# Query and key products of a linear-attention layer: seven half products in place of eight, the residual parked in memory, loops over pairs written out

## The reference, cut to what matters

```python
H, D, BS = 32, 64, 64
qkv = silu(hidden_states @ qkv_w.T).reshape(b, s, H, 3 * D)
q, k, v = split(qkv, 3)
# per head: attention inside a block with a decay, plus a decayed running state
aw = einsum('bhid,bhjd->bhij', qi, ki) * dd
out = einsum('bhij,bhjd->bhid', aw, vi) + einsum('bhid,bhde->bhie', qi * qd, state)
state = state * bd + einsum('bhsd,bhse->bhde', ki * kd, vi)
attn = rmsnorm(out, norm_w)
gate = sigmoid(hidden_states @ gate_w.T)
return gate * attn @ out_w.T
```

## Time and profile before

| | before |
|---|---|
| median of 3 runs | 5099.79 us (5098.65 to 5100.75) |
| the profiled execution's own time | 5098.89 us |
| its span | 5097.2 us |
| `linear_heads`, first product to last output product | 2950.80 to 4164.5 us of the span |
| PE busy | 4591.1 us, 90% of the span |
| DVE, POOL, ACT busy | 48%, 32%, 32% |
| mean granted TensorE clock | 0.952 of full |

### The profile page before, as it was taken

The page is one execution under the profiler, slowest core; times in us unless marked ns, Lnnn a source line. Parts: engine busy times, 40 slices in busy tenths (PEclk is TensorE's granted clock), DMA queues, the critical chain, the costliest instruction groups (busy, mean ns, idle before and its releaser), DMA issues. The chain is left out here.

```text
span 5097.2 us, 66465 instructions
## 1 busy us (share of the span) xinstructions
PE 4591.1 (90%) x26178; PEld 2569.4 (50%) x26180; DVE 2425.6 (48%) x3642; ACT 1625.0 (32%) x2792; POOL 1638.8 (32%) x1066
## 2 busy tenths in 40 slices
PE   6359997899999999969999689999999989699996
PEld 3124443433333333246666356666665658666663
DVE  7865888367777777751222313333333344512222
ACT  5414443211555556632111122222222210321110
POOL 2010000002888885215555211111111110155553
PEclk8679998999999999989999899999999999899998
DMA  2000000100000000047888610000000022479987
GB/s 74 0 15 7 7 0 35 35 0 1 1 2 1 1 1 1 6 148 222 256 259 258 148 62 32 23 30 32 32 23 31 23 83 88 157 213 257 258 258 195
DMA packets 237588, 417.72 MB, mean 82 GB/s; under 512 B 31472, under 2 KB 119536, under 8 KB 237296
## 3 DMA queue, kind: packets, MB, share of 16 engines
q1 hardware_dynamic: 179952, 270.89, 16.0%
q0 software_dynamic: 57344, 142.64, 11.5%
HBM read 297.53 MB, written 115.93 MB: 81 GB/s over the span
## 5 line engine op out<-in xcount | busy, mean ns | idle before, releaser
L2387 PE MATMUL linb_pr_ps<-lin_z,linb_wt 128*128 128x512 f32 x1536 | 679.4, 596 | 17.0 <-POOL linb_slope_own L2357 17.0
L1557 ACT ACTIVATE attc_prob<-attc_ps 128x512 f32<-128x512 f32 x1024 | 547.8, 597 | 298.9 <-PE attc_ps L1473 288.7
L1589 DVE TENSOR_REDUCE attc_peak<-attc_ps 128x1 f32<-128x512 f32 x768 | 490.5, 682 | 204.8 <-PE attc_ps L1481 204.8
L1444 POOL TENSOR_TENSOR attc_acc<-attc_acc,attc_prob 128x2048 f32<-128x2048 f32 x120 | 543.4, 4528 | 40.3 <-ACT attc_prob L1557 26.4
L1481 PE MATMUL attc_ps<-att_k,att_q 32*128 32x512 f32 x1536 | 492.0, 641 | 0.0
L2387 PEld LDWEIGHTS linb_pr_ps<-lin_z,linb_wt 128*128 128x128 f32 x1536 | 286.9, 192 | 343.5 <-issue 326.3
L1473 PE MATMUL attc_ps<-att_q,att_k 32*128 32x512 f32 x2048 | 459.7, 589 | 0.0
L2563 DVE SCALAR_TENSOR_TENSOR linb_gated<-linb_osb,linb_norm_w,linb_proj 128x512 f32<-128x512 f32 x64 | 94.4, 1474 | 668.0 <-ACT linb_osb L2490 668.0
L2364 POOL TENSOR_TENSOR linb_sq<-linb_osb 128x512 f32<-128x512 f32 x64 | 70.2, 1096 | 1040.5 <-ACT linb_osb L2490 1040.5
L1493 PE MATMUL attc_ps<-attc_prob,att_v 128*32 128x256 f32 (+1 forms) x3472 | 310.4, 429 | 0.4 <-ACT attc_prob L1557 0.4
L1074 DVE TENSOR_TENSOR_SCAN ssmb_state<-ssmb_decay,ssmb_bu 128x2048 f32<-128x2048 f32 x64 | 280.7, 4413 | 54.3 <-PE ssmb_y_ps L927 29.4
(11 more groups left out here) (463 smaller groups left out, 7655.5 us busy)
## 6 DMA issues: line engine op xcount, KB each, us to landing
moe1w_wgu<-in_L_ffn_gate_up_proj SPq DMA_DIRECT2D x32, 1536.0 KB
moe2w_wgu<-in_L_ffn_gate_up_proj SPq DMA_DIRECT2D x32, 1536.0 KB
moe1w_wd<-in_L_ffn_down_proj SPq DMA_DIRECT2D x32, 512.0 KB
gated_features<-linb_gated SPq DMA_DIRECT2D x64, 256.0 KB, 2.3
moe2w_wd<-in_L_ffn_down_proj SPq DMA_DIRECT2D x32, 512.0 KB
linc_gt<-gated_features SPq DMA_DIRECT2D x7, 2048.0 KB, 8.2
linb_wt<-in_L_attn_b_qkv_w SPq DMA_DIRECT2D x16, 768.0 KB, 4.7
residual_rows<-residual SPq DMA_DIRECT2D x8, 1024.0 KB, 4.3
```

Of the source, the lines that this page charges most:

```text
L1444: pool.tensor_tensor(to, before, prob[:, U % NP, :, :], ALU.add).then_inc(pool_done, 2 if at % HALF == 1 else 1)
L1557: nc.scalar.activation(prob[:, U % NP, h, :], ps[:, bank_of(("score", U, h)), :], ACT.Exp).then_inc(exp_done, 1)
L1589: V.tensor_reduce(peak[:, w // TT % 2, i % QH, h, b:b + 1], ps[:, bank_of(("peak", U, h)), :], axis=AX.X, op=ALU.max).then_inc(mx_used, 1)
L2387: last = nc.tensor.matmul(pr_ps[:, use % 2, :], wt[:, b, kind, k, :], z[:, k, t * NB:(t + 1) * NB], start=(k == 0), stop=(k == DT - 1))
```

## The change

Let A be the weights of a pair: two block rows (query weights, key weights) by two block columns (input features 0 to 255, 256 to 511). Let B be the features: two block rows by two block columns (token block 2x, token block 2x+1). Queries and keys of two token blocks are the four blocks of A·B. The code before computes them as eight half products (each two matmuls of 512 columns, four PE records). The code after computes them as seven, by the scheme with four sums on each side (s1 to s4 of weights, t1 to t4 of tokens) and five sums behind.

- The weight sums are four tensor_tensor of 256 columns per pair on POOL, ahead of its squares of quarter 0. The token sums are eight of 1024 columns, once, on DVE. They are kept where `g.X` was: SP writes the residual to DRAM at the start, and reads it back when the last pair's products are done, between the saves of pair 14 and those of pair 15.
- Per x (0, 1): ACT copies p1 out of PSUM and takes one block out with Silu. DVE makes five sums of 512 columns (`u2`, `u3`, `kB`, `kA`, `qB`), each of one PSUM bank and one tile. ACT then applies Silu to three blocks in place, from on-chip memory. PE's products wait for these sums where they reuse or add to a bank.
- `pr_ps` has three banks, `o_ps` one instead of two.
- Quarter 0 carries the value pieces, quarter 1 the gate pieces and the tables, quarters 2 and 3 the seven products for x = 0 and 1 (two ahead of `additions`, five behind). The first quarter of a pair waits for the last in-place Silu.
- All loops over pairs are written out on every engine and SP; waits have constants.

```diff
-        PIECES = KINDS * TC
+        PIECES = 2 * TC + 2 * 7
+        PRODUCTS = ("p1", "p6", "p2", "p7", "p5", "p4", "p3")
+        SUMS = ("u2", "u3", "kB", "kA", "qB")
...
-            with eng.Fori(0, PAIRS_L // 2 - 1) as r:
-                body(r * 2, r, 0, True)
-                body(r * 2 + 1, r, 1, True)
-            body(PAIRS_L - 2, PAIRS_L // 2 - 1, 0, True)
-            body(PAIRS_L - 1, PAIRS_L // 2 - 1, 1, False)
+            for n in range(PAIRS_L):
+                body(n, n // 2, n % 2, n + 1 < PAIRS_L)
...
+            load(0, 0)
+            sp.dma_start(x_rows, g.X[:, :, :]).then_inc(x_spilled, 16)
+            load(1, 1)
...
+                if n + 1 == PAIRS_L:
+                    sp.wait_ge(x_spilled, 16)
+                    sp.wait_ge(pr_done, PAIRS_L * PIECES)
+                    sp.dma_start(g.X[:, :, :], x_rows).then_inc(x_back, 16)
...
+            def weight_sums(n, b):
...
+                pool.tensor_tensor(s1, a21, a22, ALU.add).then_inc(w_summed, 1)
+                pool.tensor_tensor(s3, a11, a21, ALU.subtract).then_inc(w_summed, 1)
+                pool.wait_ge(w_summed, 4 * n + 1)
+                pool.tensor_tensor(s2, s1, a11, ALU.subtract).then_inc(w_summed, 1)
+                pool.wait_ge(w_summed, 4 * n + 3)
+                pool.tensor_tensor(s4, a12, s2, ALU.subtract).then_inc(w_summed, 1)
...
+            def product(bank, left, right, fresh):
+                for k in range(HK):
+                    last = nc.tensor.matmul(pr_ps[:, bank, :], left[:, k, :], right[:, k, :],
+                                            start=(fresh and k == 0), stop=(k == HK - 1), skip_group_check=not fresh)
+                last.then_inc(pr_done, 1)
...
+                if "p1" in some:
+                    pe.wait_ge(pr_out, n * FROM_BANKS + (2 * TC + 2 if x else 2 * TC - 1))
+                    product(one, a11, b11, True)
+                if "p6" in some:
+                    pe.wait_ge(w_summed, 4 * n + 4)
+                    pe.wait_ge(z_summed, 4 * x + 4)
...
+                    product(two, s2, t2, True)
+                if "p2" in some:
+                    pe.wait_ge(pr_out, n * FROM_BANKS + 2 * TC + 2 * x + 1)
+                    product(one, a12, b21, False)
+                if "p7" in some:
+                    pe.wait_ge(added, after_sum(n, x, "u2"))
+                    product(two, s3, t3, False)
+                if "p5" in some:
+                    if x:
+                        pe.wait_ge(added, after_sum(n, 0, "qB"))
+                    product(three, s1, t1, True)
+                if "p4" in some:
+                    pe.wait_ge(added, after_sum(n, x, "u3"))
+                    product(two, a22, t4, False)
+                if "p3" in some:
+                    pe.wait_ge(added, after_sum(n, x, "kB"))
+                    product(three, s4, b22, False)
...
                 for q in range(TC):
                     keys_first(n, b, q)
-                    if more:
-                        piece(q, 0, n + 1, r + b, 1 - b)
+                    if more and q < 2:
+                        piece(q + 2, 0, n + 1, r + b, 1 - b)
+                    elif more:
+                        seven(n + 1, 1 - b, q - 2, PRODUCTS[0:2])
                     additions(n, b, q)
...
+                    elif more:
+                        seven(n + 1, 1 - b, q - 2, PRODUCTS[2:])
                     outputs(n, b, q)
...
+            def seven_out(n, b, x):
+                act.wait_ge(pr_done, after_product(n, x, "p1"))
+                if n or x:
+                    act.wait_ge(added, (2 * n + x) * len(SUMS))
+                nc.scalar.copy(p1[:, :], pr_ps[:, 0, :]).then_inc(pr_out, 1)
+                act.wait_ge(pr_done, after_product(n, x, "p2"))
+                nc.scalar.activation(proj[b][:, 0, tokens(2 * x)], pr_ps[:, 0, :], ACT.Silu).then_inc(pr_out, 1)
+                for name, kind, t in (("kB", 1, 2 * x + 1), ("kA", 1, 2 * x), ("qB", 0, 2 * x + 1)):
+                    act.wait_ge(added, after_sum(n, x, name))
+                    nc.scalar.activation(proj[b][:, kind, tokens(t)], proj[b][:, kind, tokens(t)], ACT.Silu).then_inc(qk_out, 1)
...
+            def sums(n, b, x, some):
+                if "u2" in some:
+                    dve.wait_ge(pr_done, after_product(n, x, "p6"))
...
+                    V.tensor_tensor(u2[:, :], pr_ps[:, 1, :], p1[:, :], ALU.add).then_inc(added, 1)
+                if "u3" in some:
+                    dve.wait_ge(pr_done, after_product(n, x, "p7"))
+                    V.tensor_tensor(u3[:, :], pr_ps[:, 1, :], p1[:, :], ALU.add).then_inc(added, 1)
...
+                    V.tensor_tensor(proj[b][:, 1, tokens(2 * x + 1)], pr_ps[:, 2, :], u3[:, :], ALU.add).then_inc(added, 1)
...
+                    V.tensor_tensor(proj[b][:, 1, tokens(2 * x)], pr_ps[:, 1, :], p1[:, :], ALU.add).then_inc(added, 1)
...
+                    V.tensor_tensor(proj[b][:, 0, tokens(2 * x + 1)], pr_ps[:, 2, :], u2[:, :], ALU.add).then_inc(added, 1)
...
+                    if more and q >= 2:
+                        sums(n + 1, 1 - b, q - 2, ("u2",))
                     update(n, q)
+                    if more and q >= 2:
+                        sums(n + 1, 1 - b, q - 2, SUMS[1:])
```

More of the change, by code:

```diff
@@ L2325, in _ @@
                 sp.dma_start(g.y_dram[1][i * P:(i + 1) * P, :], nothing[:, :]).then_inc(cleared, 16)
[L2326 to L2331, removed]
+            for n in range(PAIRS_L):
+                if n + 2 < PAIRS_L:
+                    reload(n, n % 2)
+                if n + 1 == PAIRS_L:
+                    sp.wait_ge(x_spilled, 16)
+                    sp.wait_ge(pr_done, PAIRS_L * PIECES)
+                    sp.dma_start(g.X[:, :, :], x_rows).then_inc(x_back, 16)
                 for q in range(TC):
-                    save(PAIRS_L - 2 + b, q)
+                    save(n, q)
             for b in range(2):
@@ L2369, in _ @@
             pool.sem_inc(sq_done, 2)
-            over_pairs(pool, body)
+            weight_sums(0, 0)
+            over_pairs(body)
         @block.tensor
@@ L2386, in piece @@
                     for k in range(DT):
-                        last = nc.tensor.matmul(pr_ps[:, use % 2, :], wt[:, b, kind, k, :], z[:, k, t * NB:(t + 1) * NB],
-                                                start=(k == 0), stop=(k == DT - 1))
+                        last = nc.tensor.matmul(bank, wt[:, b, kind, k, :], z[:, k, tokens(t)], start=(k == 0), stop=(k == DT - 1))
                 last.then_inc(pr_done, 1)
+            def product(bank, left, right, fresh):
[3 more added lines that the diff above has]
+                last.then_inc(pr_done, 1)
@@ new lines, in seven @@
+            def seven(n, b, x, some):
+                a11, a12, a22 = wt[:, b, 0, 0:HK, :], wt[:, b, 0, HK:DT, :], wt[:, b, 1, HK:DT, :]
+                b11, b21, b22 = z[:, 0:HK, tokens(2 * x)], z[:, HK:DT, tokens(2 * x)], z[:, HK:DT, tokens(2 * x + 1)]
+                s1, s2, s3, s4 = (wsum[:, j, :, :] for j in range(4))
+                t1, t2, t3, t4 = (zsum[:, x, j, :, :] for j in range(4))
+                one, two, three = range(3)
+                if "p1" in some:
[5 more added lines that the diff above has]
+                    if x:
+                        pe.wait_ge(added, after_sum(n, 0, "kA"))
+                    else:
+                        pe.wait_ge(pr_out, n * FROM_BANKS + 2 * TC)
+                    product(two, s2, t2, True)
[6 more added lines that the diff above has]
+                if "p5" in some:
+                    if x:
+                        pe.wait_ge(added, after_sum(n, 0, "qB"))
[6 more added lines that the diff above has]
+                    product(three, s4, b22, False)
@@ L2440, in _ @@
             pe.wait_ge(consts, N_CONSTS)
-            for kind in range(KINDS):
+            for kind in (2, 3):
                 for t in range(TC):
                     piece(kind, t, 0, 0, 0)
+            for x in range(2):
+                seven(0, 0, x, PRODUCTS)
             def body(n, r, b, more):
@@ L2489, in quarter_out @@
                 act.wait_ge(osb_used, m + 1)
-                nc.scalar.copy(osb[:, q % 2, :], o_ps[:, q % 2, :]).then_inc(o_out, 1)
-            act.sem_inc(pr_out, 2)
+                nc.scalar.copy(osb[:, q % 2, :], o_ps[:, :]).then_inc(o_out, 1)
             act.sem_inc(kt_done, 1)
@@ L2499, in _ @@
             table(0, 0)
-            for kind in range(KINDS):
+            for kind in (2, 3):
                 for t in range(TC):
                     piece_out(kind, t, 0, 0)
+            for x in range(2):
+                seven_out(0, 0, x)
             def body(n, r, b, more):
@@ L2506, in body @@
                     keys_out(n, q)
[L2507 to L2509 removed]
+                    if more and q < 2:
+                        if q == 1 and n:
+                            act.wait_ge(gated_done, n * TC)
                         for t in range(TC):
[L2511 to L2512 removed]
```

(12 more changed lines are left out.)

87 lines of the change are left out of this document (66 added, 21 removed).

## The result

The kernel after takes 5027.99 us (median of 4 runs, 5025.78 to 5029.77) against 5099.22 of before: ratio 0.9858, 95% interval 0.9846 to 0.987. The forecast was 5028. The profiled execution took 5025.78 us, its span is 5024.1, 73.1 less than before. Of the runs further down, one of the kernel with doubled sums took 5381.75 us at a mean granted clock of 0.855, against 0.951 in the others of that kernel, and is left out of its median.

A forecast was written before the change was run, and what follows sets the result against it. PE's instructions were taken to bound the head stage: 5098.89 - 54.9 (products) - 17.3 (loops) + 0.7 (prologue) = 5027.4, plus 0.9 for the median, 5028 us. Own range 5020 to 5040; 8-in-10 range 5018 to 5048.

The forecast's parts named there:

- Products: On PE in the head stage, two half products fewer per pair save 3.43 us, 54.9 us over 16 pairs.
- Loops: PE's hardware-loop turns in the head stage cost 17.3 us, 12.0 of it idle; written-out loops save it all.
- that rival: PE's "issue" gap at loop turns stays in written-out code: 17.3 us come back, 5046 us; chance 0.05.
- End of the prologue: PE's 0.8 us wait before pair 0 is uncovered and grows by one sum, +0.7 us.
- Covers: In seven-product quarters, other PE work hides each wait for sums by 0.5 to 1.7 us; priced zero.
- DVE: Ten sums a pair add 6.9 us to DVE's 23 of now 70 us, not near PE.
- POOL: Four weight sums take about 3 us in quarter 0, needed over 36 us later; price zero.
- Parking: Residual write to DRAM takes 11 us, at most 17, read back ends at 13 to 19; covered, price zero.
- The price of a rate half as high: Rival in the last pair: a read back at half the slow rate holds it, about 12 us, 5040; chance 0.04.
- Quarters: Start to start, quarter 0 takes 19.0 us, quarter 1 18.2, quarters 2 and 3 16.5 each; a pair 70.4.
- Clock: With no gaps on PE, the stage has no lowered-clock stretch but the first; clock 1.00.
- The rival that three cycled banks make the clock swing: Within the small-waits rival: waits of three PSUM banks show as a clock under 1.00; 5060 to 5071, chance 0.08.

The follow-up runs named there:

- the two mixed kernels: Kernel before with PE's loop kept, all others written out: 5100.21 us, ratio 1.000; with PE's loop alone written out: 5082.57 us, ratio 0.9965.
- The kernel with three sums: Kernel after with each of DVE's five sums preceded by two more of the same size: 5080.07 us, ratio 0.9962.

## Why the prediction was right

- *Products*: 54.9 us forecast. Measured 51.6 for 15 pairs by the difference of two kernels, and 54.9 for all 16 by adding the product back.
- *Loops*: 17.3 us forecast from 15 pairs against their undisturbed length; 17.25 measured with the loops alone written out. The gap did not stay, so that rival is excluded. That it is PE's own turn was not known before; the two mixed kernels show it.
- *End of the prologue*: +0.7 forecast; PE's wait there grew from 0.8, for ACT's last piece, to 1.5, for the last in-place Silu.
- *Covers*: all held. I laid them out for the slowest DVE and gave u2 1.0 us to spare; it has 1.5 in the quarter shown: the gating there starts 0.7 us into the quarter and not 1.5, and takes 0.75 and not 1.54, so that u2 waits only for its product. The 0.5 us at the pair boundary is 0.65, of which 0.10 is hand-over, a cost that I took as zero. The kernels with more sums show that these were the margins: the boundary's ends just short of twice the work, the products' between two and three times.
- *DVE*: I took 6.9 us more a pair; it was 4.9 (27.91 against 22.98). The ten sums cost 0.69 each as forecast; the gating was slow less often (last section). Of 160 sums only one ran beside an instruction of POOL, at 692 ns, so that they hold 0.69 beside POOL is hardly tested.
- *POOL*: price zero, right. A weight sum is 722 ns, 2.9 us for four; I said about 3.
- *Parking*: price zero, right, but its sizes were off. I took 11 us, 17 at most; it was 15.6 out and 16.2 back. The rate of 382 GB/s was not what was wrong. On the way out the weights of two pairs were in flight beside the 4 MB, and on the way back the first microseconds are slow (last section). The save of quarter 0 landed 18.8 us into the last pair, and the gating that needs its buffer came at 23.7. The price of a rate half as high, 12 us, was not tested as such; with twice the bytes it was 5.7.
- *Quarters*: I expected 19.0, 18.2, 16.5, 16.5 and got 18.76, 18.42, 16.70, 16.48. The pair's 70.36 was right, but these four add up to 70.2. Quarters 0 and 3 have two records fewer than 1 and 2 (no state product for the first chunk, no update for the last). My 18.2 was a quarter 3, so 1 and 2 came out 0.2 us short. And my 3.63 us for a value piece counted the length of the last record; in the kernel before the quarter with the values takes 18.98 us against 18.42 for the one ahead of it, 0.14 us a piece, so a value piece is 3.57 and quarter 0 came out 0.24 too long.
- *Clock*: no lowered stretch in the pairs, as forecast. The rival that three cycled banks make the clock swing did not come true: 1.00 over 914.68 us. In the kernel after PE has no idle between groups for it to act on. The kernel with three sums has: up to 0.7 us of idle at p4 and at the pair boundary, and its clock from pair 0 to pair 15 is 1.00 too.

## What to carry to other kernels

Where one engine is busy in every microsecond of a stage, price a change as instructions times their start-to-start distance on it, and spend the rest of the work on whether each new wait has another instruction of that engine in front of it. Take the loss of a hardware loop as the difference between the real and the undisturbed length of its passes: it holds the idle turn and the clock that falls behind it. Written-out code matters on the engine that sets the pace; on the others it changed nothing here. Do not take the time of one transfer from issue to landing as the time of the next: what else is in the queues and the slow start are in it, and the second of two transfers can cost less.

## What the runs showed of the hardware

- PE's loop turn costs 1.8 to 2.4 us of idle, 12.0 in six, and in three of six turns a quarter at a granted clock of 0.91 behind it, 1.6 us more. Which turns differ from run to run, and the length of the gap does not decide it: in the kernel before a gap of 1.81 us had a slow quarter behind it (19.81), one of 2.23 had none (18.20). The total was the same 17.3 in the kernel before and with the others' loops written out.
- 15.6 and 16.2 us from issue to landing are not the rate of a 4 MB transfer. On the way out, 365 GB/s moved from 2935.5 to 2951.0, the weights of two pairs included, and 406 to 411 from 2940. On the way back, 216 GB/s from 4065 to 4068 and 402 from 4071 to 4074. Of the two reads issued back to back the second landed 11.4 us behind the first, 367 GB/s; the clearing moved at 382.
- DVE's gating and POOL's square read the same tile at nearly the same moment, and one of the two is slow each time. Before, POOL starts at 3443.60 and takes 1.04, DVE at 3443.65 takes 1.54. After, DVE starts at 3553.44 and takes 0.75, POOL at 3553.55 takes 1.54. The Trainium skill, SBUF — State Buffer, "Who interferes with whom", says that whoever issues first holds the shared ports for the whole instruction and blocks the other; these rows agree. By the start times that the profile records it does not always come out so. In 44 of the 128 gatings of both kernels DVE starts 43 to 45 ns ahead of POOL and is the slow one all the same:

```profile
3025.80 1.63 DVE L2698 SCALAR_TENSOR_TENSOR linb_gated<-linb_osb,linb_norm_w,linb_proj 128x512 f32<-128x512 f32 x1 [10.87 <-ACT linb_osb L2588]
3025.85 1.04 POOL L2398 TENSOR_TENSOR linb_sq<-linb_osb 128x512 f32<-128x512 f32 x1 [17.44 <-ACT linb_osb L2588]
```

DVE kept its 0.75 us in the 56 cases in which it started 108 ns or more ahead, and lost it in the 28 in which POOL started first. So which of the two holds the ports changes somewhere between 45 and 108 ns of DVE's lead. The slow gatings were 57 of 64 before and 15 of 64 after; no row of PE waits for one.
